# A conv, attention and expert kernel: taps picked before the turn, their product split into high and low rows, expert weights loaded in thirds

## The reference, cut to what matters

```python
# x: (8, 192, 16, 16);  K = 7, offsets: two diagonals, the middle column, the middle row
feat_n = feature / max(norm over channels, eps)          # feature = group norm of x
corr = stack([sum over channels(feat_pad[:, :, r:h+r, c:w+c] * feat_n) for r, c in offsets])   # 28 taps
x = x + (einsum('bchw,oc->bohw', concat([feature, corr]), conv_w) + conv_b)
t = tokens(x)                                            # 8 x 256 tokens of 192
t = t + causal_attention(layernorm(t), wq, wk, wv)
gate = layernorm(t) @ Wg.T + bg                          # best expert of 8 for each token
t = t + W3[e] @ (silu(W1[e] @ f) * (W2[e] @ f))          # F = 469
```

## Time and profile before

| | us |
|---|---|
| median of 3 runs | 234.52 |
| lowest, highest | 233.04, 238.59 |
| the profiled execution | 233.54 |
| its span in the trace | 231.7 |

### The profile page before, as it was taken

How to read it: one execution, slowest core, us unless ns; L and a number is a source line. 1 busy time by engine, 2 the same in 40 slices (tenths; PEclk the granted TensorE clock), 3 DMA queues, 4 the chain that set the end, 5 groups by cost and what they waited for, 6 DMA issues and landing times.

```text
span 231.7 us, 4547 instructions
## 1 busy us (share of the span) xinstructions
PE 209.1 (90%) x1331; PEld 182.4 (79%) x1331; DVE 171.4 (74%) x559; ACT 113.9 (49%) x244; POOL 105.3 (45%) x133
## 2 busy tenths in 40 slices
PE   6999799989899969998888799999999999999950
PEld 3686588968799958887665688898999999999940
DVE  3577897768399769699877789997767686868640
ACT  2276585175499697996640134343343333343410
POOL 4245756545439996896665103223131313131221
PEclk9999999999999999999999999999999999999995
DMA  6992247665730663647212332332001000000000
GB/s 218 366 350 87 83 126 187 170 219 165 252 135 0 237 234 117 221 188 259 81 52 63 80 86 70 93 83 78 21 14 37 17 34 20 34 17 22 33 20 0
DMA packets 16343, 26.46 MB, mean 114 GB/s; under 512 B 3795, under 2 KB 12673, under 8 KB 15424
## 3 DMA queue, kind: packets, MB, share of 16 engines
q1 hardware_dynamic: 14448, 22.65, 30.7%
q0 software_dynamic: 1872, 3.52, 4.4%
HBM read 19.76 MB, written 6.76 MB: 114 GB/s over the span
## 4 chain that ended last, share of the span: by engine, by line
PE 59%; DVE 16%; POOL 6%; issue 6%; DMA 6%; ACT 5%; POOLq 1%; DVEq 0%; ACTq 0%
PE bank L1468 8%; PE bank L1146 4%; PE bank L1333 4%; PE bank L1150 4%; PE bank L1149 4%; PE bank L1148 4%; PE bank L1147 4%; PE bank L1429 4%; PE bank L1469 3%; DMA stage<-in_w_all 2%; PE bank L1446 2%; PE bank L1192 2%; DMA taps_sb<-near_rows 2%; DMA out_rows<-yo,rows 1%; PE bank L1141 1%
## 5 line engine op out<-in xcount | busy, mean ns | idle before, releaser
L498 POOL DMA_INDIRECT out_rows<-yo,rows x23 | 23.2, 1011 | 76.9 <-DVE yo L1107 61.5
L1468 PE MATMUL bank<-wall,HH 128*128 (+1 forms) x88 | 28.1, 374 | 0.3 <-issue 0.3
L667 ACT ACTIVATE HH<-bank 128x512 fp32r<-128x512 f32 x23 | 13.8, 599 | 27.8 <-PE bank L1429 27.7
L1089 DVE TENSOR_TENSOR gh<-gh,bank 128x470 f32<-128x470 f32 x23 | 14.8, 645 | 14.5 <-PE bank L1150 14.4
L673 ACT ACTIVATE FH<-bank 128x256 fp32r<-128x256 f32 x23 | 8.9, 385 | 27.5 <-PE bank L1446 27.5
L1469 PE MATMUL bank<-wall,HL 128*128 (+1 forms) x88 | 22.1, 251 | 0.0
L1146 PE MATMUL bank<-wall,FH 128*128 (+1 forms) x46 | 19.3, 419 | 1.6 <-DVE FL L1092 1.6
L464 POOL DMA_INDIRECT token_rows<-rows,posi x16 | 16.9, 1055 | 7.3 <-issue 4.0
L670 ACT ACTIVATE gh<-bank 128x470 f32<-128x470 f32 x23 | 13.0, 565 | 13.1 <-PE bank L1150 13.1
L1278 PE MATMUL bank<-mH 128*128 128x512 f32 x73 | 19.3, 400 | 0.0
L1084 DVE TENSOR_TENSOR HL<-bank,HH 128x512 fp32r<-128x512 f32 x23 | 15.9, 691 | 3.6 <-ACT HH L667 3.4
(11 more groups left out here) (247 smaller groups left out, 647.4 us busy)
## 6 DMA issues: line engine op xcount, KB each, us to landing
stage<-in_w_all SPq DMA_DIRECT2D x7, 1324.0 KB, 5.7
rows<-token_rows SPq DMA_DIRECT2D x23, 98.0 KB, 2.0
near_rows<-gram SPq DMA_DIRECT2D x8, 243.0 KB, 3.2
xcm<-in_x_cm SPq DMA_DIRECT2D x2, 768.0 KB, 8.3
rows<-in_x_tm SPq DMA_DIRECT2D x1, 1536.0 KB, 14.0
stage<-in_w_all SPq DMA_DIRECT2D x4, 331.0 KB, 4.0
token_rows<-emptyt SPq DMA_DIRECT2D x3, 294.0 KB, 4.2
taps_sb<-near_rows SPq DMA_DIRECT2D x8, 103.0 KB, 2.1
```

The lines of the kernel that those rows point to most:

```text
L498: pool.indirect_dma_start(out=out, out_offset=bass.IndirectOffsetOnAxis(ap=rows[:, j, C + 2:C + 3].bitcast(U32), axis=0), in_=yo[:, par], ...
L1468: nc.tensor.matmul(dst[:, 0:2 * C], HH[:, 1 - par, k], w(0, P, c0, c0 + 2 * C), start=(k == 0), stop=False)
```

## The change

Four things are changed.

1. The taps' transfer now lands in a new tile `reached`. ScalarE (`keep_taps`, at step b+4 between `high_pixels` and `copy_norms`) picks the 28 taps with weights out of the 103 by four strided copies, each of which writes four copies side by side into a 128 wide `taps`. `turn_taps` waits for that. `conv_taps` becomes fp32r: rows 0 to 63 of the turned taps are high parts, rows 64 to 127 become low parts by a new DVE instruction (`low_taps`, 64x256, after `take_gram` in the queue), and `wtap` has high, low, high, low rows, so that one product gives all four combinations. The matmul with `place` goes; DVE gets two 32x192 subtractions at step 3.
2. POOL fills `taps` first (now 128x512), PE's first `keep_busy` waits for that fill alone and does 6 matmuls, not 3.
3. Each expert from the second on is loaded in three transfers with semaphores of their own, and each third waits only for the reader of its own old content (`wall_lo_a` is raised after POOL's first part). ACT waits for a third at a time.
4. In the expert stage, `low_weights` pieces 4 and 5 of expert 6 move to slots -1 and 0, those of expert 7 to slots 4 and 5 alone, and the pieces 0 to 3 of expert 7 come a slot earlier. `fill(8)` becomes `fill(5)`.

```diff
-        taps = sb("taps_sb", [P, 2, HALVES, TAPS], ctx=early)
-        tapsT = sb("taps_t", [TAPS, 2, PIX], ctx=early)
-        wtap = sb("wtap", [TAPS, C], ctx=early)
+        reached = sb("reached", [P, 2, HALVES, REACHED], ctx=early)
+        taps = sb("taps_sb", [P, 2, HALVES, P], ctx=early)
+        tapsT = sb("taps_t", [P, 2, PIX], F32R, early)
+        wtap = sb("wtap", [P, C], F32R, early)
...
+            def weights_in(e, part):
+                c = PARTS[part]
+                sp.dma_start(stage[:, e % 2, c], w_all[e][:, c]).then_inc(stage_in[e % 2][part], 16)
...
                 if b >= 2:
-                    sp.wait_ge(taps_t_ready, b - 1)
+                    sp.wait_ge(taps_kept, b - 1)
...
-                sp.dma_start(taps[:, b % 2, :, 0:REACHED], of[:, :, 0:REACHED]).then_inc(taps_in[b % 2], 16)
+                sp.dma_start(reached[:, b % 2], of[:, :, 0:REACHED]).then_inc(taps_in[b % 2], 16)
...
             for e in range(2, EXPERTS):
+                sp.wait_ge(wall_lo_a, e - 1)
+                weights_in(e, 0)
+                sp.wait_ge(wall_q, e - 1)
+                weights_in(e, 1)
                 sp.wait_ge(wall_lo, e - 1)
-                sp.wait_ge(wall_q, e - 1)
-                weights_in(e)
+                weights_in(e, 2)
...
+            def keep_taps(b):
+                sc.wait_ge(taps_in[b % 2], 16 * (b // 2 + 1))
+                sc.wait_ge(filled, 1)
+                if b >= 2:
+                    sc.wait_ge(taps_t_ready, b - 1)
+                to = taps[:, b % 2].rearrange("p h (g n) -> p h g n", g=4)
+                for d, (first, pitch) in enumerate(DIRECTIONS):
+                    of = reached[:, b % 2, :, first:first + (KERNEL - 1) * pitch + 1:pitch].rearrange("p h (g i) -> p h g i", g=1)
+                    ins = nc.scalar.activation(to[:, :, :, KERNEL * d:KERNEL * (d + 1)], of.to_broadcast([P, HALVES, 4, KERNEL]), ACT.Copy)
+                ins.then_inc(taps_kept, 1)
...
+                if i >= LAG:
+                    keep_taps(i - LAG)
                 if 2 <= i < IMAGES + 2:
                     copy_norms(i - 2)
...
+            def low_taps(b):
+                ve.wait_ge(taps_copied, b + 1)
+                at = slice(2 * QUARTER, P)
+                nc.vector.tensor_tensor(tapsT[at, b % 2], bank[5][at, 0:PIX], tapsT[at, b % 2].bitcast(F32), ALU.subtract).then_inc(taps_low, 1)
...
                 if 2 <= i < IMAGES + 2:
                     take_gram(i - 2)
+                if LAG <= i < IMAGES + 2:
+                    low_taps(i - LAG)
...
+                    for q in (1, 3):
+                        at = slice(QUARTER * q, QUARTER * (q + 1))
+                        nc.vector.tensor_tensor(wtap[at], c1("taps")[at], wtap[at].bitcast(F32), ALU.subtract)
...
-                pe.wait_ge(taps_copied, b + 1)
+                pe.wait_ge(taps_low, b + 1)
...
-            pe.wait_ge(filled, 4)
-            keep_busy(3, taps[:].rearrange("p b h c -> p (b h c)"))
+            pe.wait_ge(filled, 1)
+            keep_busy(6, taps[:].rearrange("p b h c -> p (b h c)"))
...
-                if 0 <= j < 3:
+                if 0 <= j < 2:
                     low_weights(EXPERTS - 2, (2 * j, 2 * j + 1))
-                elif 3 <= j < 6:
-                    low_weights(EXPERTS - 1, (2 * j - 6, 2 * j - 5))
+                elif 2 <= j < 6:
+                    low_weights(EXPERTS - 1, ((0, 1), (2, 3), (4,), (5,))[j - 2])
...
                 if j == 0:
-                    fill(8)
+                    fill(5)
```

More of the change, by code:

```diff
@@ L104 @@
 _at = 0
-for _n, _w in (("gm", 4 * CA), ("cf", 2 * C), ("taps", C), ("place", TAPS), ("beside", P), ("wq", 4 * CA), ("wk", 4 * CA), ("wv", 2 * C), ("wvt", 4 * CA)):
+for _n, _w in (("gm", 4 * CA), ("cf", 2 * C), ("taps", C), ("beside", P), ("wq", 4 * CA), ("wk", 4 * CA), ("wv", 2 * C), ("wvt", 4 * CA)):
     S1[_n] = (_at, _at + _w)
@@ L242, in build @@
         cm_in = [sem(f"cm_in{g}") for g in range(len(GANGS))]
-        stage_in = [sem("stage_in0"), sem("stage_in1")]
+        first_in = sem("first_in")
+        stage_in = [[sem(f"stage_in{par}{part}") for part in range(3)] for par in range(2)]
+        wall_lo_a = sem("wall_lo_a")
+        PARTS = (slice(0, W12), slice(W12, 2 * W12), slice(2 * W12, STAGE))
         empty_out = sem("empty_out")
@@ L333, in _ @@
                 taps_from(b)
-            weights_in(1)
+            for part in range(3):
+                weights_in(1, part)
             for e in range(2, EXPERTS):
+                sp.wait_ge(wall_lo_a, e - 1)
+                weights_in(e, 0)
+                sp.wait_ge(wall_q, e - 1)
+                weights_in(e, 1)
                 sp.wait_ge(wall_lo, e - 1)
-                sp.wait_ge(wall_q, e - 1)
-                weights_in(e)
+                weights_in(e, 2)
             def load_first_tile(e):
@@ L370, in _ @@
         def _(pool):
+            nc.gpsimd.memset(taps[:].rearrange("p b h c -> p (b h c)"), 1.0).then_inc(filled, 1)
             nc.gpsimd.memset(half_c[:], -0.5).then_inc(filled, 1)
@@ L546, in weights_hi @@
                     sc.wait_ge(conv_taken, IMAGES)
-                sc.wait_ge(stage_in[e % 2], 16 * (e // 2 + (1 if e % 2 else FIRST_PARTS)))
+                if e == 0:
+                    sc.wait_ge(first_in, 16 * FIRST_PARTS)
+                else:
+                    sc.wait_ge(stage_in[e % 2][part], 16 * ((e + 1) // 2))
                 if part == 0:
@@ L645, in _ @@
                     nc.scalar.activation(beside[:], c1("beside"), ACT.Copy).then_inc(beside_ready, 1)
-                    nc.scalar.activation(cfH[:], c1("cf"), ACT.Copy).then_inc(wsplit_hi, 1)
-                    sc.wait_ge(wtap_ready, 1)
-                    nc.scalar.activation(wtap[:], bank[5][0:TAPS, 0:C], ACT.Copy).then_inc(wtap_copied, 1)
+                    nc.scalar.activation(cfH[:], c1("cf"), ACT.Copy)
+                    nc.scalar.activation(wtap[:], c1("taps"), ACT.Copy).then_inc(wsplit_hi, 1)
                 if i == 2:
@@ L1115, in _ @@
                     table_slots()
+                    low_weights(EXPERTS - 2, (4,))
                 elif j == 0:
@@ L1118, in _ @@
                     norm_slot(1, 1, 1)
+                    low_weights(EXPERTS - 2, (5,))
                     ffn_step(j, 0, False, False, True, 2)
@@ L1340, in _ @@
             group_sums(1)
-            pe.wait_ge(small1_in, 16)
-            nc.tensor.matmul(bank[5][0:TAPS, 0:C], c1("place"), c1("taps"), start=True, stop=True).then_inc(wtap_ready, 1)
             for i in range(1, IMAGES + LAG):
@@ L1505, in lay_out @@
     offs += [(i, KERNEL - 1 - i) for i in range(KERNEL)] + [(REACH, i) for i in range(KERNEL)]
-    taps, place = np.zeros((P, C), f), np.zeros((P, TAPS), f)
-    taps[:len(offs)] = conv_w[:, C:].T
-    taps[len(offs)] = conv_b
-    for n, (r, cx) in enumerate(offs):
-        place[n, (r - REACH) * SIDE + cx - REACH + EDGE] = 1
-    place[len(offs), REACHED] = 1
+    taps = np.zeros((4, QUARTER, C), f)
+    taps[:, :len(offs)] = conv_w[:, C:].T
+    taps[:, len(offs)] = conv_b
+    taps = taps.reshape(P, C)
+    centre = [(r - REACH) * SIDE + cx - REACH + EDGE for r, cx in offs]
+    assert centre == [first + i * pitch for first, pitch in DIRECTIONS for i in range(KERNEL)]
     px = np.arange(P) % SIDE
     beside = (np.abs(px[:, None] - px[None, :]) <= REACH).astype(f)
-    s1 = [a_b0(cols_a_bb(gm)), a_bb(conv_w[:, :C].T), taps, place, beside,
+    s1 = [a_b0(cols_a_bb(gm)), a_bb(conv_w[:, :C].T), taps, beside,
           a_b0(cols_a_bb(wq.T)), a_bb(cols_a_bb(wk.T)), a_bb(wv), a_b0(cols_a_bb(wv.T))]
```

35 lines of the change are left out of this document (15 added, 20 removed).

## The result

The changed kernel takes 241.61 us (median of 4 runs, 239.90 to 241.96), the kernel before, run beside it, 235.15 us (233.04 to 238.59). The ratio is 1.0347, with a 95% interval of 1.0308 to 1.0387. The prediction was 232.8 us, within 2% of before; the change is slower, and outside the range.

What follows compares the result with a forecast made beforehand. It took a ring of waits through PE, ACT, DVE and POOL to bound the convolution stage, ACT attention, PE the experts. Terms -0.2 + 1.9 - 1.8 - 1.1 = -1.2 us gave 232.8 us, range 229.6 to 235.9.

Steps and rivals of the forecast that it cites:

- The start: First matmuls and group sums: PE starts 1.0 us earlier, `group_sums(1)` moves by -0.2 us, between -0.7 and +0.9.
- Convolution stage: Image loop up to `project(0)`: later taps products against PE time saved, sum +1.9 us, bounds -3 to +4.
- The product starts at 43.5, 1.0 later, and gives 0.65 back: Step 7 of the image loop: `conv_taps` waits for `low_taps`, queued behind `take_gram`; net +0.35 us.
- The two new DVE subtractions at step 3: Convolution stage: at most 0.35 us each, pushing `take_gram` of step 4 by another 0.4 us.
- The wait for the transfer in step 9, for image 5: Convolution stage: ACT waits for taps landing 3.78 us after issue; `copy_norms` 1.6 us late, `low_xt(0)` 2.1.
- The rival that it decides everything: Convolution stage, 17%: late taps hold ACT, `copy_norms`, gram and next taps, 0.9 us per step; 235, at worst about 239.
- So the wait goes, -1.8: Attention stage: expert 3's first third lands before ACT needs it, ending its 1.80 us wait; bounds -2.0 to -0.3.
- The thirds change nothing: Attention stage rival, 8%: three queues of small pieces compete, landing takes over 6 us, the 1.8 wait stays; 234.1.
- Expert stage: Fewer filling matmuls, 0.49 us usable, and moved `low_weights` pieces, 0.2 + 0.4 saved: -1.1 us, between -1.4 and -0.4.
- The 0.04: Whole kernel: chance of slower by over 2%, if late taps hold ACT in every step 4 to 9 and thirds give nothing.
- The bound of +4: Convolution stage: the upper bound of its +1.9 us term, if the transfers land later still.
- a ring: Convolution stage: `conv_taps`, ACT, DVE, POOL, PE's `near_norms`, `conv_taps` again; any delay of `conv_taps` delays the stage.

Runs made afterwards that it cites:

- thirds_hold: Kernel before with experts loaded in thirds, and GpSimd's second low part of experts 3 and 4 held until VectorE finished its share; 236.2 us, ratio 1.0102.
- after_warm: Changed kernel with four 128-column filling matmuls ahead of `conv_taps` for images 0 to 5 and two more `keep_busy` in step 3; ratio 1.0134.
- after_swap: Changed kernel with VectorE taking the centre weights' low parts before those of the taps' weights in step 3; 240.92 us, ratio 1.0338.
- after_no_low: Changed kernel without VectorE's low rows of the turned taps, so the product waits for ScalarE's copy alone; 234.19 us, ratio 1.0016.
- thirds_only: Kernel before with the expert loads in thirds and nothing else; 235.0 us, ratio 1.0012.
- hold2_ffn: Kernel before with thirds, expert-stage edits, and GpSimd's low parts of experts 3, 4 and 5 held until VectorE's share is done; 229.33 us, ratio 0.9833.
- rest_only: Kernel before with all of the change except the taps part; 234.4 us, ratio 0.9967.
- hold_ffn: Kernel before with thirds, expert-stage edits, and GpSimd's second low part of experts 3 and 4 held; 233.66 us, ratio 0.9991.

## Why the prediction was wrong

**The start.** Predicted -0.2 between -0.7 and +0.9; measured +0.3: inside the bounds, with the other sign. The second group sums came 0.5 us earlier, as worked out (12.19 for 12.68), but the first `near_gram` waits for pixels that are normalized with the first group sums, which came 1.76 us later, and began at 14.07 instead of 13.74. And +0.3 may make the new start look better than it is. `near_gram(3)` began at 24.8 to 25.0 us in five of the seven profiled kernels with the old start, at 26.2 in before and 26.5 in thirds_hold, where the five filling matmuls behind the first group sums took 5 us instead of 3.5; in the seven kernels with the new start it began at 26.1 to 27.3. By the medians of these, 24.96 and 26.53, the new start would cost 1.6 us; that is an estimate from one execution of each kernel, and no kernel changed the start alone.

**Convolution stage: the step that failed.** Predicted +1.9 between -3 and +4; measured +8.7.
- "The product starts at 43.5, 1.0 later, and gives 0.65 back" was right as a mechanism and in its first number: 0.8 to 1.2 later for images 0 to 4. The 0.65 was mis-sized. The new product holds PE for 0.31 us (36.71 to 37.01 in after_warm) for 0.23 predicted, and the 0.88 for the old one was read in a step where what followed had waited for ScalarE (57.18); in before it held PE for 0.62 to 0.76 us where nothing was waited for (29.61 to 30.23, 37.82 to 38.58, 42.48 to 43.24). So 0.3 to 0.45 us an image is given back. Taking VectorE out between turn and product shortened the stage by 7.4 us (35.05 to 27.69), which shows where the loss began.
- "The two new DVE subtractions at step 3 (at most 0.35 each)" had the right price, 0.71 for both. Missing was that two old ones behind them grew from 0.35 to 1.10 and 1.19 us. They met GpSimd's `spread`: both ended 0.2 us behind it, and after_swap put another subtraction in the same place, which took 1.11 us. No run held `spread` back to see the time. With the clock held the stage was at most +3.75, twice the predicted sum.
- The term that was absent is the clock. The prediction had seen the half-rate matmuls at the start and used the clock only there. It called any delay of `conv_taps` a delay of the stage and never asked what PE's clock does when PE waits more in a loop. That was at least 4.95 us, more than half of the loss. It could have asked: in the earlier trace rows PE was busy 42.8 of 46 us at clock 1.00, and the forecast lowered its work and raised its waits. The Trainium skill (TensorE: Matmul & The Clock Gate, HAM oscillation — how this bites in real kernels) describes a relative of this: a wait for a transfer in each turn of a loop puts the engine back to its lower level each time. The trace agrees in what came of it, 0.50 from 35 to 50 us, but not in the kind of wait: here the waits before the fall were for VectorE and ScalarE, none over 1.2 us, and the engine fell once in the stage. The prediction cited another section of that page, and only for the start.
- The wait for the transfer in step 9, for image 5, did not show in the changed kernel; such waits were real, and hidden by the larger loss (in after_no_low 3.18 us for image 4 and 1.14 for image 5). The rival that it decides everything fell.

**Attention stage.** Predicted -1.8; the wait for expert 3 went as worked out (-1.94, in every kernel with thirds). The step that failed is the sentence "So the wait goes, -1.8, and POOL and DVE, which followed ACT there, go with it". An engine off the path came earlier and met VectorE's gate and its subtraction: +2.8 us in thirds_only, and +3.9 in after, where 1.1 of it went with the lower clock behind the collision. thirds_hold and hold2_ffn show that the collision is what begins it: without it XH 5 to XH 6 is back at 7.93 and 7.94 us. It could have been read from the trace of before, in two lines that the prediction had looked past:

```profile
70.47 2.21 POOL L434 TENSOR_TENSOR wall<-stage,wall 128x940 fp32r<-128x940 f32 x1
...
71.29 2.38 DVE L837 TENSOR_TENSOR wall<-stage,wall 64x940 fp32r<-64x940 f32 x1
```

The same operation took 1.14 us at 88.35 in before. 71.29 plus 2.38 is 73.67; GpSimd ended at 72.68, and 1.0 later VectorE. One duration in the earlier trace rows, POOL's 2.76, is such a collision too: alone it is 1.84. Likewise the rival "The thirds change nothing" was right in its sum (1.0012) by another mechanism than the one it gave.

**Expert stage.** Predicted -1.1, measured -1.1, term by term.

**Chances.** Faster, same and slower had 0.11, 0.85 and 0.04. The 0.04 rested on one mechanism; two that were left out, the clock and the blocking, each moved more than any term of the sum. The bound of +4 for a stage in which a ring grows was not a bound.

## What to carry to other kernels

When an edit puts a wait on the engine that does the matmuls, price it twice: once as the wait, and once at the lower clock for what follows, and look whether the engine gets less to do in the stretch while its waits grow, as here (43 matmuls in 10 us instead of 62). When a transfer or a copy comes earlier, list what the freed engines do earlier, and look for VectorE and GpSimd subtracting from SBUF at the same time: two durations of one operation, 1.14 and 2.38, are the sign. Then a wait that keeps them apart can be worth more than the load that came sooner (2.85 us of one step, against 1.94). But weigh the whole against doing neither: here the thirds with all their waits showed no gain over the single load. And take a price from a row where nothing waits: the 0.88 us of the old product had a wait in it.

## What the runs showed of the hardware

- **VectorE and GpSimd block each other for whole instructions.** A 128 x 8 operation on VectorE with both inputs in SBUF took 1.63 us instead of about 0.2 while GpSimd's subtraction ran, and ended 0.04 us after it. Two took 3.92 us across two such subtractions. VectorE's operations with an input in PSUM kept their durations beside the same GpSimd work (in thirds_hold L812, 0.42 us at 74.39, and two of L928, 0.76 us at 82.57, against 0.42 and 0.76 elsewhere). The Trainium skill (SBUF — State Buffer, SBUF: two separate sides) says this of VectorE operations with two SBUF inputs beside a GpSimd operation that reads SBUF: the first to start holds the port pair for the whole instruction. The traces agree.
- **The clock fell with PE still busy in pieces.** In the changed kernel no single wait of PE's matmuls between 25 and 35 us was longer than 1.2 us; PE was busy for 6.2 of 10 us (8.3 in before), and from 35 to 50 us the clock was 0.50. In after_warm four 128-column filling matmuls a step (1.07 us together at 30.1) went with a clock of 1.00 through the stage. It also fell without the taps part: rest_only had 0.83 from 90 to 100 us, where PE was busy for 8.1 of 10 us, and hold2_ffn 0.72 from 25 to 30 us.
- **A granted clock below 1 may cost little.** With that fall hold2_ffn's stage was 0.7 us longer than that of hold_ffn, which has the same code there (27.0 and 26.3); in after_no_low and after_swap a fall inside step 5 of attention, while PE waited, left the step at 10.8 us, as in thirds_only at clock 1.00. In the changed kernel, where 0.50 lasted from 35 to 50 us in the ring of the image loop, it cost 4.95 or more.
